# A two-layer vision-transformer tower on one core: norms and feed-forward by halves, another form of the normalising instruction, and small work moved between steps and engines

## The chip, the cores and the metric

The kernel runs on one core of a Trainium2 chip. A core has TensorE (matmuls and transposes), VectorE, ScalarE, GpSimd and SyncE, which here only issues DMAs. Each engine has its own instruction stream and runs it in order; they wait for one another on semaphores. The metric is the device time of one execution in microseconds.

## What is computed

Sixteen images of 1024 tokens, 29 features each, pass through a token embedding, a multi-head attention with a group norm in front (8 heads of 64, "layer 0"), a feed-forward with GELU, a second attention (8 heads of 16, "layer 1") and a routed feed-forward with 16 experts and a capacity of 1.2. A layer norm without weights stands before each of the four. The reference, cut to this:

```
def _layernorm(x, axis=-1, eps=1e-05):
    m = jnp.mean(x, axis=axis, keepdims=True)
    v = jnp.var(x, axis=axis, keepdims=True)
    return (x - m) / jnp.sqrt(v + eps)
...
    h = _L0_tok_ref(x, L0_tok_W)
    h = h + _L0_attn_ref(_layernorm(h, axis=-1), L0_attn_gn_w, L0_attn_gn_b, L0_attn_wq, L0_attn_bq, L0_attn_wk, L0_attn_bk, L0_attn_wv, L0_attn_bv, L0_attn_wo, L0_attn_bo)
    h = h + _L0_ffn_ref(_layernorm(h, axis=-1), L0_ffn_W1, L0_ffn_b1, L0_ffn_W2, L0_ffn_b2)
    h = h + _L1_attn_ref(_layernorm(h, axis=-1), L1_attn_Wq, L1_attn_Wk, L1_attn_Wv, L1_attn_bq, L1_attn_bk, L1_attn_bv, L1_attn_Wo, L1_attn_bo)
    h = h + _L1_ffn_ref(_layernorm(h, axis=-1), L1_ffn_switch_w, L1_ffn_switch_b, L1_ffn_expert_w, L1_ffn_expert_b)
    return h
```

## The kernel before

A batch is one image: 1024 tokens as 8 tiles of 128 tokens by 128 channels. The program is a pipeline over batches. A *segment* holds layer 0 of one batch, layer 1 of the batch before it and the routed feed-forward (`switch`) of the one before that, and near its end the embedding of the next one (`embed`). The segments are `first`, `second`, `loop` (13 executions of one hardware loop), `penult` and `final`; only `first` and `final` do one layer alone.

The clock of a segment is the *step*. A *unit* is one head and one half of the queries (512): 8 steps, one for each tile of 128 keys (`kt`). In a loop segment 32 units make 256 steps: four units of layer 0, then layer 1 and layer 0 by turns, then four of layer 1. In each step TensorE computes one tile of row maxima for a unit some 18 steps ahead (`max_tile`, L884) and one tile of scores (`scores`, L910 and L912); ScalarE takes the exponential into `pr` (L1143); VectorE reduces the tile of maxima (L1630). The maxima and the scores have two PSUM banks each. At `kt` 2, 3, 5 and 6 TensorE multiplies the exponentials of the unit before with the values. For layer 0 it does so with the high bf16 half of the exponentials (L929) and with a *low part* (L930), the difference in bf16, which `lo_parts` (L506) makes two key tiles at a time: GpSimd does it at `kt` 2, 4 and 6 and, for the last two tiles, at `kt` 0 of the next unit (`lo_done` counts them; `values0` waits for all four). GpSimd also divides the outputs by the softmax sums (`normalize`).

Everything else is *beside* work: generators (`mlp`, `embed`, `switch`, `late`, `more_heads`, `more_values`) that yield the step at which their next piece is due. Each engine runs the same generators in its own stream, so the tables `mlp_slots`, `embed_slots` and `switch_slots` set where each piece stands among the steps of every engine. The matmuls of this work share two PSUM banks (`glue`), given out by turns in the order of the tables (`glue_plan`); a piece waits until the one two before it in the plan has been read.

A norm has three pieces. VectorE takes the statistics of eight tiles (`norm_stats`: eight bn_stats, a link through a semaphore, eight bn_aggr). GpSimd makes the reciprocal root (`rstd`, L1236 and L1237: an addition and a power on 128x8). VectorE applies it (`norm_apply`, L1425: eight tensor_scalar with two scalar columns, mean and root):

```
ins = dve.tensor_scalar(dst[:, t, :], tokens[:, t, :], mv[:, s, t, 0:1], rs[:, s, t:t + 1],
                        ALU.subtract, ALU.mult)
```

Norm 0 is that of the embedding (tile `stage`, result in `on`), norms 1 and 2 those of layer 0's result and of the feed-forward's (tile `h`), norm 3 that in front of the router (tile `hm`). The result is turned on TensorE (`z_turn`, L708). In a loop segment the pieces stand at these steps: norm 3 at 24 and 27; the router's `logits` 36, `rank` 44, `place` 50 (L1593 to L1599: the weight of each token's expert, and eight instructions on `hm`); norm 0 at 184 and 187; group norm `gn` 192 to 199 (`xn`, L1475 to L1478); `copy_hm` 216; `attn0` by halves at 226 and 235 (L791; L1432 adds it to `h`); norm 1 at 236 and 238; `ffn_h` 246 and 247 (GELU, L1090); `ffn_o` 249 and 250; norm 2 at 251 and 253. `residual0` and `residual1` are additions of 128x1024 on GpSimd (L1247, L1240). L1437 makes the low part of a projection, L1449 that of a value chunk, L1620 adds an expert's result, L825 are the value matmuls of layer 1.

## Time and profile before

| | us |
|---|---|
| median of 3 runs | 6807.82 |
| lowest and highest | 6796.63, 6813.67 |
| the profiled execution, its time | 6804.59 |
| its span, first to last instruction | 6802.8 |
| mean granted TensorE clock | 0.951 of 2.4 GHz |

A window view cuts the span and gives each engine's busy time in each piece; the clock in it is the mean granted clock, where 1.00 is 2.4 GHz and 0.50 is 1.2 GHz. A wait is named as engine, tile and line that waited, then what released it. Iteration 3 is the execution of the loop segment from 1585.11 to 1994.61 us; its steps are counted by the starts of the score matmul L912, step 0 at 1585.11.

### The profile page before, as it was taken

What the parts mean: (1) busy time and instruction counts of PE and PEld (TensorE: products, weight loads), DVE (VectorE), ACT (ScalarE), POOL (GpSimd) and SP (SyncE); (2) the same over time, 40 slices, a digit from 0 to 9 for tenths busy, and PEclk for the clock granted to TensorE, in tenths of its full rate; (3) what the DMA queues carried; (4) which work ended last, traced back from release to release, by engine and by line L of the source; (5) the groups of instructions that cost most, each with busy time, mean ns of one, the idle gap of its engine ahead of it and who ended that gap; (6) DMA issues with size and microseconds to landing.
All of it is one profiled execution on the core that took longest, in us unless ns stands there. A gap on an engine that the chain in (4) does not pass through costs nothing.

```text
span 6802.8 us, 126677 instructions
## 1 busy us (share of the span) xinstructions
PE 6049.1 (89%) x40167; PEld 4017.5 (59%) x40167; DVE 4474.2 (66%) x11034; ACT 3218.6 (47%) x6321; POOL 2516.2 (37%) x2135
## 2 busy tenths in 40 slices
PE   6788898998989889898998989989898998989986
PEld 4556665665656666565665656666565665656543
DVE  4456676776757667576776767767676676767664
ACT  2345545444444444554544444454544544454531
POOL 3534433433333333333433333343333433333300
PEclk7899999999999999999999999999999999999987
DMA  2121221221122121211212222121211212222110
GB/s 59 41 67 41 58 51 29 63 51 46 46 53 49 39 52 42 59 42 38 63 42 49 49 50 49 44 50 45 59 42 38 63 34 57 49 50 44 25 30 9
DMA packets 98046, 317.01 MB, mean 47 GB/s; under 512 B 27782, under 2 KB 32854, under 8 KB 87126
## 3 DMA queue, kind: packets, MB, share of 16 engines
q1 hardware_dynamic: 97366, 308.41, 19.6%
q8 instruction: 370, 6.06, 0.4%
q14 instruction: 310, 2.54, 0.1%
HBM read 57.19 MB, written 41.94 MB: 15 GB/s over the span
## 4 chain that ended last, share of the span: by engine, by line
issue 44%; POOL 25%; PE 22%; DVE 4%; ACT 2%; DMA 2%; SPq 1%; POOLq 1%; DVEq 0%; ACTq 0%
POOL pr_lo L506 21%; PE bank L884 4%; PE bank L912 3%; PE bank L945 3%; POOL on L1265 2%; PE bank L910 2%; PE bank L870 2%; PE bank L929 2%; PE bank L930 2%; DMA stacks<-parts 1%; DVE mxh L1630 1%; PE bank L719 1%; PE bank L818 1%; PE bank L708 1%; PE bank L955 1%
## 5 line engine op out<-in xcount | busy, mean ns | idle before, releaser
L1630 DVE TENSOR_REDUCE mxh<-bank 128x1 f32<-128x512 f32 x4096 | 2789.0, 688 | 1797.3 <-PE bank L884 1779.6
L1143 ACT ACTIVATE pr<-bank 128x512 f32<-128x512 f32 x4096 | 2418.4, 598 | 2723.7 <-PE bank L912 2679.9
L884 PE MATMUL bank<-stacks 128*128 128x512 f32 x4096 | 2221.3, 543 | 348.4 <-DVE mxh L1630 233.9
L506 POOL TENSOR_TENSOR pr_lo<-pr 128x1024 bf16<-128x1024 f32 x1024 | 1944.7, 1902 | 911.4 <-ACT pr L1143 909.1
L912 PE MATMUL bank<-stacks 65*128 65x512 f32 (+1 forms) x4096 | 1673.2, 409 | 27.7 <-ACT pr L1143 27.7
L884 PEld LDWEIGHTS bank<-stacks 128*128 128x128 f32 x4096 | 799.9, 195 | 1090.2 <-DVE mxh L1630 757.7
L929 PE MATMUL bank<-v,pr 128*128 128x129 bf16 x8192 | 1063.5, 222 | 94.6 <-POOL pr_lo L506 93.3
L930 PE MATMUL bank<-v,pr_lo 128*128 128x129 bf16 x8192 | 1051.1, 220 | 0.0
L929 PEld LDWEIGHTS bank<-v,pr 128*128 128x128 bf16 x8192 | 779.5, 98 | 393.1 <-issue 346.3
L1265 POOL TENSOR_TENSOR on<-on,o_r 128x128 f32<-128x128 f32 x512 | 205.4, 401 | 2045.5 <-DVE on L1660 2045.4
L912 PEld LDWEIGHTS bank<-stacks 65*128 65x128 f32 (+1 forms) x4096 | 800.2, 195 | 261.4 <-ACT pr L1143 94.4
L910 PE MATMUL bank<-stacks 128*128 128x512 f32 x2048 | 833.3, 407 | 0.2 <-ACT pr L1143 0.2
L930 PEld LDWEIGHTS bank<-v,pr_lo 128*128 128x128 bf16 x8192 | 805.2, 98 | 0.0
L870 PE MATMUL bank<-ewT,mx 128*128 128x512 f32 x1024 | 565.2, 638 | 91.7 <-DVE hm L1620 44.8
L1620 DVE SCALAR_TENSOR_TENSOR hm<-bank,wgt,hm 128x128 f32<-128x128 f32 x2048 | 571.1, 342 | 50.7 <-PE bank L870 50.7
L945 PE MATMUL bank<-pr,v 128*32 128x512 f32 x4096 | 573.6, 636 | 0.0
L910 PEld LDWEIGHTS bank<-stacks 128*128 128x128 f32 x2048 | 401.6, 196 | 133.8 <-ACT pr L1143 90.5
L955 PEld LDWEIGHTS bank<-fold,oT 128*128 128x128 f32 x2048 | 270.6, 199 | 63.0 <-ACT oT L1160 50.5
L870 PEld LDWEIGHTS bank<-ewT,mx 128*128 128x128 f32 x1024 | 183.9, 200 | 205.6 <-DVE hm L1620 68.7
L1040 ACT ACTIVATE parts<-bank,cols 128x512 fp32r<-128x512 f32 x256 | 176.4, 689 | 224.0 <-PE bank L719 213.0
L955 PE MATMUL bank<-fold,oT 128*128 128x32 f32 x2048 | 266.3, 275 | 12.6 <-ACT oT L1160 12.6
L1273 POOL TENSOR_TENSOR on<-on,o_r 128x64 f32<-128x64 f32 x256 | 75.4, 295 | 538.1 <-DVE on L1672 538.0
(170 smaller groups left out, 4925.2 us busy)
## 6 DMA issues: line engine op xcount, KB each, us to landing
stacks<-parts SPq DMA_DIRECT2D x384, 512.0 KB, 6.5
stacks<-parts_d SPq DMA_DIRECT2D x224, 128.0 KB, 3.0
parts_d<-mx SPq DMA_DIRECT2D x16, 1024.0 KB, 4.5
stacks<-parts_d SPq DMA_DIRECT2D x224, 64.0 KB, 2.8
stage<-in_pe SPq DMA_DIRECT2D x16, 512.0 KB, 7.8
stacks<-mrow SPq DMA_DIRECT2D x512, 2.0 KB
parts_d<-on SPq DMA_DIRECT2D x16, 512.0 KB, 5.2
parts_d<-stage SPq DMA_DIRECT2D x16, 512.0 KB, 6.2
```

The costliest lines, as they stand in the source:

```text
L506: return eng.tensor_tensor(low_of(u, kt - 1).rearrange("p a b -> p (a b)"), w, hi, ALU.subtract)
L870: mm(bank[:, :], mT[:, t * P:(t + 1) * P], ewT[:, 4 * q:4 * q + 4, :].rearrange("p e f -> p (e f)"), start=True, stop=True).then_inc(fille ...
L884: mm(maxb[k % 2][:, :], qs[:, t * P:(t + 1) * P], ks[:, g * HALF:(g + 1) * HALF], start=True, stop=True).then_inc(max_filled.sem, 1)
L910: mm(bank[:, :], kA[:, head % 2, kk], qA[:, head % 2, q], start=True, stop=False)
L912: mm(bank[:, :], k_stack(layer, head)[0:last, kk], q_stack(layer, head)[0:last, q], start=(layer == 1), stop=True).then_inc(score_filled.s ...
L929: mm(dst, hi, v0[:, head // 2 % 2, kt, head % 2, 0:w], start=(kt == 0), stop=False)
L930: last = mm(dst, lo, v0[:, head // 2 % 2, kt, head % 2, 0:w], start=False, stop=(kt == T - 1))
L945: last = mm(obank[n % 2][QUAD * r:QUAD * (r + 1), :], v1[:, kt, col:col + QUAD], pr[:, at % 2, kt, :], start=(j == 0), stop=(j == 1))
L955: last = mm(obank[n % 2][:, QUAD * t:QUAD * (t + 1)], oT[:, t * P:(t + 1) * P], fold[:, :], start=True, stop=True)
L1143: act.activation(pr[:, at % 2, kt, :], score[k % 2][:, :], ACT.Exp, scale=SCALES[layer]).then_inc(exp_done.sem, 1)
L1620: ins = dve.scalar_tensor_tensor(hm[:, t, :], bank[:, e * P:(e + 1) * P], wgt[:, t, 4 * q + e:4 * q + e + 1], hm[:, t, :], ALU.mult, ALU.add)
L1630: dve.tensor_reduce(mxh[:, layer, n // 2, n % 2:n % 2 + 1], maxb[k % 2][:, :], AX_X, ALU.max)\
```

## The change

Norms and feed-forward go by halves of four tiles. `norm_stats`, `rstd` and `norm_apply` take a half `g`, and each half has its own steps. `mlp` becomes two generators, one for each half: the first half's norm 1, turn, GELU, second matmul and norm 2 stand at steps 228 to 242, the second half's at 237 to 251. Norm 0 stands at 184 and 186 (statistics, on VectorE a step later) and 188 and 190 (apply), norm 3 at 22 and 24, 26 and 28; the group norm ends at 203 instead of 199. `residual1` goes by halves as well; `copy_hm` moves from 216 to 210, `residual0` stays at 243.

The normalising instruction becomes a scalar_tensor_tensor with one scalar column (the mean); the root comes as a second tensor, one column broadcast over 128.

GpSimd's small pieces stand one or two steps later than the pieces on which they wait, and its prefix chain moves from `rank` (44) to `place` - 4 (50); `place` moves to 54. On VectorE the router's work is cut over more steps.

The last low part of each of the first four units of layer 0 in a segment (`LEADING`) moves from GpSimd to the head of the next unit's first step on VectorE, with a semaphore of its own (`lo_last`).

```diff
-    at = {"copy": -40, "oT0.3.0": -34, "attn0.0": -30, "oT0.3.1": -23, "attn0.1": -21, "ln1": -20, "z1": -18, "zT1.0": -13,
-          "zT1.1": -12, "ffn_h0": -10, "ffn_h1": -9, "ffn_o0": -7, "ffn_o1": -6, "ln2": -5, "z2": -3}
-    return {name: LAST[kind] + step for name, step in at.items()}
+    halves = ({"oT0.3": -34, "attn0": -30, "ln1": -28, "z1": -26, "zT1": -23, "ffn_h": -21, "ffn_o": -18, "ln2": -16, "z2": -14},
+              {"oT0.3": -23, "attn0": -21, "ln1": -19, "z1": -17, "zT1": -14, "ffn_h": -12, "ffn_o": -9, "ln2": -7, "z2": -5})
+    slots = {f"{name}.{g}": LAST[kind] + step for g, half in enumerate(halves) for name, step in half.items()}
+    return {"copy": LAST[kind] - 46, "res0": LAST[kind] - 13, **slots}
...
-    at = {"xT0": 179, "xT1": 180, "h0": 182, "h1": 183, "ln": 184, "z": 187, "zT0.0": 190, "zT0.1": 191, "gn": 192,
-          "gn_mean": 194, "gn_var": 197, "xn": 199, "q0.0": 204, "q0.1": 206, "k0.0": 209, "k0.1": 211, "v0c0.0": 213,
+    at = {"xT0": 179, "xT1": 180, "h0": 182, "h1": 184, "ln.0": 184, "ln.1": 186, "z.0": 188, "z.1": 190, "zT0.0": 191, "zT0.1": 193, "gn": 194,
+          "gn_mean": 196, "gn_var": 199, "xn": 203, "q0.0": 206, "q0.1": 207, "k0.0": 209, "k0.1": 211, "v0c0.0": 213,
           "v0c0.1": 215, "q1.0": 237, "q1.1": 239, "k1.0": 252, "k1.1": 254}
     return {name: LAST[kind] - 256 + step for name, step in at.items()}
...
-        at = {"oT1.0": 18, "oT1.1": 19, "attn1.0": 21, "attn1.1": 22, "ln": 24, "z": 27, "zT3.0": 31, "zT3.1": 32,
-              "logits": 36, "route": 38, "rank": 44, "place": 50, "wT0": 58, "wT1": 59, "eb0": 61, "eb1": 62}
+        at = {"oT1.0": 18, "oT1.1": 19, "attn1.0": 21, "attn1.1": 22, "ln.0": 22, "ln.1": 24, "z.0": 26, "z.1": 28, "zT3.0": 30, "zT3.1": 31,
+              "logits": 36, "route": 38, "rank": 44, "place": 54, "wT0": 59, "wT1": 60, "eb0": 62, "eb1": 63}
         first = [8 * m for m in range(8, 24)]
...
-        stats_ready = [Counts(sem(f"stats_ready{n}"), 1) for n in range(4)]
-        rstd_ready = [Counts(sem(f"rstd_ready{n}"), 1) for n in range(5)]
+        stats_ready = [Counts(sem(f"stats_ready{n}"), 2) for n in range(4)]
+        rstd_ready = [Counts(sem(f"rstd_ready{n}"), 1 if n == 4 else 2) for n in range(5)]
...
-        lo_done = Counts(sem("lo_done"), 16 * 4)
+        lo_done = Counts(sem("lo_done"), LO_DONE[-1])
+        lo_last = Counts(sem("lo_last"), LEAD)
...
-                    te.wait_ge(lo_done.sem, lo_done.at(seg.l0, 4 * (u + 1)))
+                    te.wait_ge(lo_done.sem, lo_done.at(seg.l0, LO_DONE[u + 1]))
+                    if u < LEAD:
+                        te.wait_ge(lo_last.sem, lo_last.at(seg.l0, u + 1))
...
-                    pool.wait_ge(stats_ready[n].sem, stats_ready[n].at(b, 1))
-                    s = int(n == 0)
-                    var, dst, eps, width = mv[:, s, :, 1], rs[:, s, :], pool_c[:, 1, :], T
+                    pool.wait_ge(stats_ready[n].sem, stats_ready[n].at(b, g + 1))
+                    s, ts = int(n == 0), slice(4 * g, 4 * g + 4)
+                    var, dst, eps, width = mv[:, s, ts, 1], rs[:, s, ts], pool_c[:, 1, 0:4], 4
                 link(seg, pool.tensor_tensor(dst, var, eps, ALU.add))
                 pool.tensor_tensor(dst, dst, pool_c[:, 0, 0:width], ALU.pow).then_inc(rstd_ready[n].sem, 1)
...
+            def residual1(b, g):
+                pool.wait_ge(z_ready[1].sem, z_ready[1].at(b, g + 1))
+                part = h[:, 4 * g:4 * g + 4, :]
+                biased(part, part, b2_b, 4).then_inc(res1_ready.sem, 1)
...
                 AT = switch_slots(seg.kind)
-                yield AT["ln"]
-                rstd(seg, b, 3)
-                yield AT["rank"]
+                for g in range(2):
+                    yield AT[f"ln.{g}"] + 2
+                    rstd(seg, b, 3, g=g)
+                yield AT["place"] - 4
...
+                for g in range(2):
+                    yield AT[f"ln.{g}"] + 2
+                    rstd(seg, seg.nxt, 0, g=g)
+                yield AT["gn_var"] + 2
                 rstd(seg, seg.nxt, 4)
...
+                yield AT[f"ln1.{g}"] + 1
+                rstd(seg, seg.l0, 1, g=g)
+                yield AT[f"z1.{g}"] + 1
+                residual1(seg.l0, g)
+                yield AT[f"ln2.{g}"] + 1
+                rstd(seg, seg.l0, 2, g=g)
...
+            def residuals(seg):
                 AT = mlp_slots(seg.kind)
                 yield AT["copy"]
                 if seg.l1:
                     copy_hm(seg)
-                yield AT["ln1"]
-                rstd(seg, seg.l0, 1)
-                yield AT["z1"]
-                residual1(seg.l0)
-                yield AT["zT1.0"]
+                yield AT["res0"]
                 if seg.nxt:
                     residual0(seg, seg.nxt)
...
-                    elif kt == 0 and at > 0 and units_of(seg.kind)[at - 1][0] == 0:
+                    elif kt == 0 and at > 0 and units_of(seg.kind)[at - 1][0] == 0 and units_of(seg.kind)[at - 1][1] >= LEAD:
                         lo_parts(pool, seg, at - 1, T - 1).then_inc(lo_done.sem, 1)
...
-            def norm_stats(seg, n, tokens):
+            def norm_stats(seg, n, tokens, g):
                 s = int(n == 0)
-                for t in range(T):
+                for t in range(4 * g, 4 * g + 4):
                     ins = dve.bn_stats(st[:, s, t, :], tokens[:, t, :])
                 link(seg, ins)
                 dve.memset(small[:, 7, 0:1], 0.0)
-                for t in range(T):
+                for t in range(4 * g, 4 * g + 4):
                     ins = dve.bn_aggr(mv[:, s, t, :], st[:, s, t, :])
                 ins.then_inc(stats_ready[n].sem, 1)

-            def norm_apply(b, n, tokens):
+            def norm_apply(b, n, tokens, g):
                 s, dst = int(n == 0), z0_s if n == 0 else z
-                dve.wait_ge(stats_ready[n].sem, stats_ready[n].at(b, 1))
-                dve.wait_ge(rstd_ready[n].sem, rstd_ready[n].at(b, 1))
-                for g in range(2):
-                    for j in range(4):
-                        t = 4 * g + j
-                        ins = dve.tensor_scalar(dst[:, t, :], tokens[:, t, :], mv[:, s, t, 0:1], rs[:, s, t:t + 1],
-                                                ALU.subtract, ALU.mult)
-                    ins.then_inc(z_ready[n].sem, 1)
+                dve.wait_ge(stats_ready[n].sem, stats_ready[n].at(b, g + 1))
+                dve.wait_ge(rstd_ready[n].sem, rstd_ready[n].at(b, g + 1))
+                for t in range(4 * g, 4 * g + 4):
+                    ins = dve.scalar_tensor_tensor(dst[:, t, :], tokens[:, t, :], mv[:, s, t, 0:1],
+                                                   rs[:, s, t:t + 1].broadcast_to([P, C]), ALU.subtract, ALU.mult)
+                ins.then_inc(z_ready[n].sem, 1)

...
+                yield AT[f"attn0.{g}"] + 1
+                if g == 0:
+                    dve.wait_ge(res0_ready.sem, res0_ready.at(seg.l0, 1))
+                    if seg.l1:
+                        dve.wait_ge(hm_copied.sem, hm_copied.at(seg.l1, 1))
+                add_result(seg, f"attn0.{g}", g, h, h0)
+                yield AT[f"ln1.{g}"]
+                await_drained(dve, seg, f"attn0.{g}")
+                norm_stats(seg, 1, h, g)
+                yield AT[f"z1.{g}"]
+                norm_apply(seg.l0, 1, h, g)
+                yield AT[f"ffn_o.{g}"] + 1
+                dve.wait_ge(res1_ready.sem, res1_ready.at(seg.l0, g + 1))
+                add_result(seg, f"ffn_o.{g}", g, h, h)
+                yield AT[f"ln2.{g}"]
+                await_drained(dve, seg, f"ffn_o.{g}")
+                norm_stats(seg, 2, h, g)
+                yield AT[f"z2.{g}"]
+                norm_apply(seg.l0, 2, h, g)

...
                 dve.wait_ge(prefix_ready.sem, prefix_ready.at(b, 7))
                 link(seg, dve.tensor_tensor(lg[:, :, :], oh[:, :, :], prefix[:, :, :], ALU.mult))
                 link(seg, dve.tensor_reduce(pos, lg[:, :, :], AX_X, ALU.add))
+                yield AT["place"] + 1
                 link(seg, dve.scalar_tensor_tensor(kr, pos, CAP, rp, ALU.is_lt, ALU.mult))
                 link(seg, dve.tensor_tensor(un, rp, kr, ALU.subtract))
                 dve.tensor_tensor(wgt[:, :, :], oh[:, :, :], over_e(kr), ALU.mult).then_inc(wgt_ready.sem, 1)
                 for t in range(T):
+                    if t % 4 == 0:
+                        yield AT["place"] + 2 + t // 4
                     ins = dve.scalar_tensor_tensor(hm[:, t, :], z[:, t, :], un[:, t:t + 1], hm[:, t, :], ALU.mult, ALU.add)
-                link(seg, ins)
+                    if t % 4 == 3:
+                        mark(seg, ins)
+                settle(seg)
                 for g in range(2):
                     yield AT[f"eb{g}"]
                     add_result(seg, f"{pre}eb{g}", g, hm, hm)
...
                 for step, at, layer, u, kt in steps_of(seg.kind):
+                    if kt == 0 and at > 0 and units_of(seg.kind)[at - 1] in LEADING:
+                        lo_parts(dve, seg, at - 1, T - 1).then_inc(lo_last.sem, 1)
                     tiles_due(seg, step)
...
+LEADING = [(0, u) for u in range(LEAD)]
+
+LO_DONE = [3 * min(u, LEAD) + 4 * max(u - LEAD, 0) for u in range(17)]
```

## Rows read from the trace of the kernel before

**Rows 1.** the page: busy us (share of the span) and instructions of each engine

```profile
PE 6049.1 (89%) x40167; PEld 4017.5 (59%) x40167; DVE 4474.2 (66%) x11034; ACT 3218.6 (47%) x6321; POOL 2516.2 (37%) x2135
```

**Rows 2.** windows of iteration 3: stretch, length, busy per engine, clock, DMA, GB/s

```profile
1585.11:1994.61 409.50, 371.62 (x2509) 248.30 (x2508) 279.61 (x689) 201.05 (x395) 157.34 (x133) 0.97 0.21 48
1703.02:1723.23 20.21, 20.21 (x139) 13.15 (x138) 15.84 (x41) 10.16 (x22) 8.62 (x7) 1.00 0.07 15
1624.40:1639.84 15.44, 12.26 (x109) 9.69 (x108) 14.43 (x41) 6.60 (x14) 10.06 (x8) 1.00 0.00 1
1664.02:1692.79 28.77, 25.37 (x176) 17.42 (x174) 20.22 (x43) 13.82 (x29) 10.23 (x9) 0.96 0.05 15
1860.84:1881.02 20.18, 14.66 (x62) 9.43 (x61) 15.96 (x45) 6.09 (x12) 8.37 (x8) 0.76 0.14 47
1924.99:1994.61 69.62, 55.53 (x334) 33.58 (x333) 37.20 (x110) 32.02 (x56) 14.83 (x15) 0.92 0.18 39
```

**Rows 3.** TensorE's waits in iteration 3: us in total, times, longest

```profile
PE bank L884 <- DVE mxh L1630: 14.4, 10, 5.5
...
PE bank L884 <- DMA stacks<-parts: 1.9, 1, 1.9
```

**Rows 4.** lines L1425, L1593, L1620 of the code: ns min/median/max, first and last start

```profile
L1425 DVE TENSOR_SCALAR z<-h,mv,rs x256: 337/342/348, 366.9 to 6463.0; 128x128 f32<-128x128 f32 x128
L1425 DVE TENSOR_SCALAR on<-stage,mv,rs x128: 332/336/2003, 46.5 to 5971.9; 128x128 f32<-128x128 f32 x128
...
L1593 DVE TENSOR_TENSOR lg<-oh,prefix x16: 291/1734/1744, 850.1 to 6707.5; 128x128 f32<-128x128 f32 x16
...
L1620 DVE SCALAR_TENSOR_TENSOR hm<-bank,wgt,hm x2048: 335/342/353, 880.9 to 6799.4; 128x128 f32<-128x128 f32 x187
```

**Rows 5.** groups of instructions: busy us, mean ns | idle before them

```profile
L1449 DVE TENSOR_TENSOR v<-bank,v 128x512 bf16<-128x512 f32 x128 | 87.5, 684 | 2.5 <-ACT v L1044 2.5
...
L1599 DVE SCALAR_TENSOR_TENSOR hm<-z,small,hm 128x128 f32<-128x128 f32 x128 | 35.0, 346 | 0.0
```

**Rows 6.** in order of time, steps 187 to 239: start, us, engine, line, [idle]

```profile
1866.68 6.19 DVE L1425 TENSOR_SCALAR on<-stage,mv,rs 128x128 f32<-128x128 f32 x8
...
1865.93 3.75 POOL L506 TENSOR_TENSOR pr_lo<-pr 128x1024 bf16<-128x1024 f32 x2
...
1874.56 0.79 PE L884 MATMUL bank<-stacks 128*128 128x512 f32 x1 [5.52 <-DVE mxh L1630]
...
1953.17 2.14 DVE L1425 TENSOR_SCALAR z<-h,mv,rs 128x128 f32<-128x128 f32 x8 [0.71 <-POOL rs L1237]
```

**Rows 7.** in order of time, steps 50 and 51: GpSimd, VectorE, TensorE

```profile
1665.79 1.89 POOL L506 TENSOR_TENSOR pr_lo<-pr 128x1024 bf16<-128x1024 f32 x1
...
1666.12 1.72 DVE L1593 TENSOR_TENSOR lg<-oh,prefix 128x128 f32<-128x128 f32 x1
...
1667.82 0.23 PE L929 MATMUL bank<-v,pr 128*128 128x129 bf16 x1 [2.11 <-POOL pr_lo L506]
```

**Rows 8.** in order of time, step 201: TensorE

```profile
1893.47 0.50 PE L884 MATMUL bank<-stacks 128*128 128x512 f32 x1 [1.95 <-DVE mxh L1630]
```

**Rows 9.** in order of time, step 9: TensorE

```profile
1597.99 1.16 PE L825 MATMUL bank<-wv_sb,zT 128*128 128x128 f32 x8 [0.17 <-DVE mx L1437]
```

**Rows 10.** TensorE's waits in steps 224 to 256 of iteration 3

```profile
PE bank L884 <- DVE mxh L1630: 3.0, 3, 1.5
PE bank L890 <- DVE parts L1437: 2.3, 1, 2.3
PE bank L912 <- ACT pr L1143: 1.7, 2, 1.2
PE bank L806 <- ACT mx L1090: 1.5, 1, 1.5
```

**Rows 11.** in order of time, steps 242 and 248: GpSimd, ScalarE

```profile
1957.96 2.35 POOL L1247 TENSOR_TENSOR h<-stage,on 128x1024 f32<-128x1024 f32 x1
...
1967.76 1.28 ACT L1143 ACT_TABLE_LOAD   x1
```

162 lines of the change are left out of this document (66 added, 96 removed).

## The prediction

> **What bounds the kernel now.** The page first: TensorE is busy 89% of the span, VectorE 66%, GpSimd 37% [rows 1]. That is an average over unlike stretches, so I took one execution of the main loop (iteration 3, 1585.11 to 1994.61 us, 409.5 us; 13 such executions and two cousins make most of the span), cut it at its 256 score steps and put windows over the pieces [rows 2]. In the plain steps 72 to 88 TensorE is busy 20.21 of 20.21 us at clock 1.00: nothing beside it costs anything there. The trouble is local. Steps 184 to 192, where the next batch is normalised, take 20.18 us with TensorE busy 14.66 and the clock at 0.76; steps 48 to 64 take 28.77 with 25.37 busy; steps 24 to 32 take 15.44 with VectorE busy 14.43, so there VectorE sets the pace; steps 224 to 256 take 69.62 with 55.53 busy at 0.92. TensorE's waits name the cause [rows 3]: 14.4 us for the tile maximum L1630. Tiles have two banks, so TensorE can be two tiles ahead of VectorE and no more. The bound is thus TensorE, plus each moment in which a burst on VectorE, or a late low part, outlasts that lead.
>
> **The new scalar form.** A normalising instruction on 128x128 takes 0.342 us in its median and 0.348 at most on `h`, where GpSimd is idle, but up to 2.003 on `stage` [rows 4]. Why: eight of them from 1866.68 took 6.19 us while GpSimd ran L506; eight on `h` took 2.14, so 4.05 us was standing still until L506 let go [rows 6]. The new form reads two SBUF tensors, `tokens` and the broadcast `rs`. Unhindered, its twin is L1599, a scalar_tensor_tensor from SBUF: 0.346 us [rows 5], so 0.004 x 512 = 2 us of VectorE, nothing. Does it escape the hold? Bounds: wholly (L1620, with one operand in PSUM, never over 0.353 us in 2048) or not at all (L1593, a tensor_tensor from two SBUF tensors: median 1.734, alone 0.291) [rows 4]. L1593 ended at 1667.84, 0.16 us after the L506 beside it [rows 7]. The new form has L1593's operands, so I take "not at all".
> (a) Steps 184 to 192. Of 20.18 us 5.5 are the wait for L1630 [rows 6]; clock 0.76 means 2 x 0.24 x 20.18 = 9.7 us at 1.2 GHz, worth up to 4.8 us. The halves make two bursts of four (1.05 us, 2.9 when held by one L506) with tile maxima between, which the two banks half cover. But GpSimd's order becomes low part, root, low part, root, low part, and each z half again begins when the next L506 can. Floors are VectorE's own 15.96 us with the holds kept [rows 2], 11.9 without. I take 15.7, -4.5. Bounds -1 (only the second embedding half moved) and -8.3 (20.18 to 11.9).
> (b) Steps 200 to 208. `xn` goes from step 199 to 203, where value matmuls fill TensorE while VectorE works. The wait before the tile at 1893.47 is 1.95 us [rows 8]. -1.4; bounds 0 and -1.9.
> (c) Steps 48 to 64. GpSimd stood at step 44 for the rank, so its last L506 ended at 1667.68 and TensorE waited 2.11 us for it [rows 7]. From step 50 the prefix chain has no low part behind it, as steps 48 to 55 are a layer-1 unit: -2.1 nearly sure. `place` at step 54 meets an idle GpSimd, so L1593 goes from 1.72 to 0.29 us, and its eight L1599 are split in two. Clock 0.96 over 28.77 us is 2.3 us at 1.2 GHz, worth 1.1. I take the first and the last, -3.2; bounds -2.1 and -4.6 (with L1593's 1.4).
> (d) Steps 16 to 34. Half of the `hm` statistics goes ahead to step 23, but before that TensorE waits 1.9 us for the DMA of the next stack [rows 3], issued after the maxima row of step 16, which swallows what is gained before step 21. One low part comes to VectorE at step 24, where it is nearly full [rows 2]. These cancel: 0; bounds +1.5 and -3 (VectorE rid of its holds, one and a half L506).
> (e) Last low parts of units 0 to 3 on VectorE: no row shows this there. From 0.291 us for 128 elements (L1593) and 0.684 for 512 (L1449) [rows 4, 5], 1024 make 1.21 us alone, 3.1 if held by an L506 of 1.89. It waits for the exponential of the unit's last step; queued behind it are the tile maximum and, at step 8, L1437, for which TensorE's L825 already waits 0.17 us [rows 9]. VectorE would have gone on 0.2 us earlier without it: L1437 comes 1.0 us later, +1.0. At steps 16 and 32 the low part comes about 1 us before GpSimd's and the tile maxima 1.2 us later: 0. Bounds 0 and +3.
> (f) Steps 224 to 256. Now: waits of 3.0 for tile maxima, 2.3 for L1437, 1.7 and 1.5 behind the GELU [rows 10] with a table load of 1.28 us [rows 11] before and after each half. New: the first GELU half at step 235 lies beside the attn0.1 matmuls, and w2 comes three steps after it: -1.9 of 3.2. The loads stay four. At steps 239 to 242 half bursts of both norms meet on VectorE (addition, z1.1, statistics 2.0, L1437, z2.0), so I leave the 2.3. The burst in step 254 halves and moves to 251: -0.8 and some clock, together -2.1. Against that, z2.0 is released by the same root after which GpSimd goes straight into residual0, L1247 of 2.35 us [rows 11] and an L1240 like it; with two SBUF operands z2.0 is held by the first: +2.0. copy_hm at step 210 lies in a layer-1 unit with GpSimd idle (38% busy in the loop [rows 2]), the two-instruction roots likewise: nothing. No DMA is moved. Sum -2.0; bounds +4 and -8.
> Together -4.5 - 1.4 - 3.2 + 0 + 1.0 - 2.0 = -10.1 us. 13 loops: -131. Second segment, with no switch (without c): -6.9. Penult, with no next batch (without a, b): -4.2. First and last, where a norm's chain lies open and one half can run under the other's root: -6 together, bounds 0 and -20. Total -148 from the profiled execution's 6804.59 us: 6656.5. That execution is 3.2 us under the median of 6807.82; put back, 6660.
>
> **Rivals.**
> A: the form escapes the hold, since a second operand of stride 0 may not count as a read. For it, only that L1620 is free; against, L1593. Then a is -8.3, d -2.6, f loses its +2.0: -18.5 per loop; 13 x 18.5, 21 for the two cousins and 6 are 268: 6540.
> B, no change: the holds eat the halves. a -1, b -1.4, c -2.1, e +1, f +2.7 (z2.0 held by L1247 and L1240, 4.7): -0.8 per loop: 6797.
> C, slower: the low parts stop VectorE. If each waits for an L506 (1.9) before its own 1.2, and before that for its exponential (put at 0.6), that is 3.7 us four times, 14.8 per loop against -11.1 from the other terms: +3.7, 15 times +55, with -6: 6857. It decides from 2.8 us per unit on. Against: at steps 8 and 16 GpSimd's previous L506 is over by then.
> The skill's rule on the shared interface speaks against A, as L1593 does.
>
> **Chances and range.** Forecast 0.58, A 0.20, B 0.11, C 0.11. Faster by over 0.3% (20 us, about what a measurement of this kernel can tell from no change): the forecast, A and a third of B, 0.82; within 0.3% 0.06; slower C and a little of B, 0.12. The forecast's own bounds, with terms missing in different directions, give about 6570 to 6750; the range 6540 to 6790 reaches A's time and most of the way to B, and leaves out C.
>
> **What would show it.** The normalising line's maximum on `stage`: near 1.9 us (held) or under 0.4 (A). Steps 184 to 192 near 16 us with the clock over 0.9. No L929 wait near 2 us after step 50. 64 low parts on VectorE at 1.2 us; over 2 us means C. z2.0 starting beside L1247 and held. If steps 224 to 256 still take 69 us, f was wrong; if steps 8 to 16 take over 14, e; if the clock stays at 0.76 in steps 184 to 192 although the wait shrank, half of a.

## The result and the profile after

The changed kernel takes 6751.24 us (median of 4 runs, 6740.80 to 6756.80), the kernel before 6807.56 in the same comparison: ratio 0.9916, 95% interval 0.9904 to 0.9929. It is faster, by 56 us, and inside the range, but the forecast was 148 us: by its size the prediction was wrong. The profiled execution's span is 6748.1 us at a mean clock of 0.948 (before 0.951).

The page, busy time of each engine; then windows of iteration 3 of the loop, as in [rows 2] (whole iteration, steps 8 to 16, 24 to 32, 48 to 64, 184 to 192, 224 to 256, 240 to 248):

```profile
PE 6073.5 (90%) x40167; PEld 4046.7 (60%) x40167; DVE 4525.4 (67%) x11162; ACT 3214.0 (48%) x6321; POOL 2465.6 (37%) x2215
```

```profile
1581.22:1986.76 405.54, 372.40 (x2509) 250.40 (x2508) 282.22 (x697) 200.50 (x395) 154.15 (x138) 0.97 0.21 48
1593.11:1605.79 12.68, 11.69 (x107) 9.42 (x106) 7.26 (x13) 6.35 (x13) 6.04 (x4) 1.00 0.70 197
1623.63:1640.76 17.13, 13.89 (x114) 11.55 (x112) 13.40 (x43) 7.21 (x15) 9.19 (x9) 0.90 0.00 2
...
1664.57:1691.17 26.60, 24.54 (x175) 16.90 (x174) 19.24 (x43) 13.87 (x29) 10.98 (x16) 0.99 0.06 16
...
1858.86:1876.60 17.74, 14.39 (x65) 8.05 (x64) 12.49 (x46) 5.62 (x12) 8.53 (x8) 0.90 0.15 53
...
1922.29:1986.76 64.47, 54.35 (x334) 34.87 (x333) 40.90 (x112) 32.01 (x56) 16.21 (x20) 0.93 0.19 41
1952.82:1969.59 16.77, 13.01 (x57) 7.92 (x56) 13.39 (x30) 9.68 (x15) 7.48 (x6) 0.83 0.01 2
```

The iteration fell from 409.5 to 405.5 us where 399.4 was forecast. Steps 184 to 192 took 17.7 us (20.18 before, 15.7 forecast), steps 48 to 64 26.6 (28.77), steps 224 to 256 64.5 (69.62), but steps 24 to 32 17.1 where they had taken 15.44 [rows 2]. TensorE's waits in the iteration (us in total, times, longest), to be held against [rows 3]:

```profile
PE bank L883 <- DVE mxh L1640: 14.1, 12, 3.2
...
PE bank L869 <- DVE stage L1435: 1.7, 1, 1.7
...
PE bank L742 <- DVE stage L1435: 1.1, 1, 1.1
```

The wait for the tile maximum (now L1640) didn't shrink: 14.4 before, 14.1 after. The single wait of 5.5 us in step 189 became 0.5. In its place stand 3.24 in step 25, where it had been 0.91 (and 2.02 in step 29, now gone), and 2.94 in step 244, where there was none. Two new waits name the stage addition L1435. Cut at the score steps and averaged over eleven of the 13 loop executions (the first and the last left out), a stretch at a time (us; idle is TensorE's, low is time at 1.2 GHz):

| steps | before: length, idle, low | after: length, idle, low | change | forecast |
|---|---|---|---|---|
| 0 to 16 | 23.5, 0.2, 3.3 | 24.9, 1.0, 4.6 | +1.4 | +1.0 |
| 16 to 40 | 43.3, 7.4, 0.3 | 45.4, 7.4, 6.5 | +2.1 | 0 |
| 40 to 72 | 51.8, 3.9, 4.0 | 50.3, 2.0, 4.0 | -1.5 | -3.2 |
| 176 to 200 | 43.8, 6.4, 10.2 | 42.3, 5.7, 5.9 | -1.5 | -4.5 |
| 200 to 216 | 25.2, 2.0, 0.9 | 25.0, 2.0, 0.3 | -0.3 | -1.4 |
| 224 to 256 | 68.9, 13.6, 10.7 | 64.4, 10.1, 9.0 | -4.5 | -2.0 |
| whole loop | 409.9, 37.3, 29.5 | 405.8, 32.1, 30.3 | -4.1 | -10.1 |

TensorE's idle time fell by 5.2 us a loop and its low clock not at all: it left steps 184 to 192 and turned up in steps 16 to 32. In this mean steps 184 to 192 take 18.5 us, a little more than in iteration 3. Outside the loop the second segment fell from 376.9 to 372.4 us and the last from 313.0 to 309.4, while the first (from its first score on) rose from 306.5 to 312.3 and `penult` from 399.4 to 401.0.

Then the normalising line itself (ns, minimum, median, maximum), against L1425 in [rows 4]:

```profile
L1428 DVE SCALAR_TENSOR_TENSOR z<-h,mv,rs x256: 337/346/2502, 358.8 to 6405.3; 128x128 f32<-128x128 f32 x128
L1428 DVE SCALAR_TENSOR_TENSOR on<-stage,mv,rs x128: 319/343/1059, 43.9 to 5931.6; 128x128 f32<-128x128 f32 x128
```

The maximum on `stage` is 1.06 us, neither the "near 1.9" nor the "under 0.4" of the prediction's signs, and on `h` an instruction that had never been held now stands for 2.5 us.

### The profile page after: what moved, and what is told of

It reads as the page before. It is cut to its first block, busy times and chain, and to the rows that moved or that the text cites. A ratio compares the mean times of both kernels' runs of the same rounds, so it can differ in the third digit from the quotient of the medians.

```text
span 6748.1 us, 127182 instructions
## 1 busy us (share of the span) xinstructions
PE 6073.5 (90%) x40167; PEld 4046.7 (60%) x40167; DVE 4525.4 (67%) x11162; ACT 3214.0 (48%) x6321; POOL 2465.6 (37%) x2215
## 4 chain that ended last, share of the span: by engine, by line
issue 47%; POOL 27%; PE 17%; DVE 6%; DMA 1%; POOLq 1%; ACT 1%; SPq 1%; DVEq 0%; ACTq 0%
POOL pr_lo L508 22%; PE bank L883 3%; POOL on L1264 3%; PE bank L911 2%; PE bank L869 2%; PE bank L946 2%; DVE mxh L1640 2%; PE bank L930 1%; DMA stacks<-parts 1%; PE bank L931 1%; DVE z L1428 1%; POOL rs L1235 1%; PE bank L793 1%; PE bank L909 1%; PE bank L956 1%
## 5 line engine op out<-in xcount | busy, mean ns | idle before, releaser
L1640 DVE TENSOR_REDUCE mxh<-bank 128x1 f32<-128x512 f32 x4096 | 2789.9, 687 | 1710.2 <-PE bank L883 1682.2
L508 POOL TENSOR_TENSOR pr_lo<-pr 128x1024 bf16<-128x1024 f32 x960 | 1824.3, 1901 | 1168.9 <-ACT pr L1141 1168.6
L930 PE MATMUL bank<-v,pr 128*128 128x129 bf16 x8192 | 1079.9, 224 | 54.1 <-POOL pr_lo L508 53.5
L931 PE MATMUL bank<-v,pr_lo 128*128 128x129 bf16 x8192 | 1067.7, 222 | 0.0
L1264 POOL TENSOR_TENSOR on<-on,o_r 128x128 f32<-128x128 f32 x512 | 235.3, 460 | 2015.7 <-DVE on L1670 2015.6
L869 PE MATMUL bank<-ewT,mx 128*128 128x512 f32 x1024 | 585.4, 658 | 114.1 <-DVE hm L1630 44.8
L946 PE MATMUL bank<-pr,v 128*32 128x512 f32 x4096 | 547.0, 609 | 0.0
```

The source lines that it names most:

```text
L508: return eng.tensor_tensor(low_of(u, kt - 1).rearrange("p a b -> p (a b)"), w, hi, ALU.subtract)
L869: mm(bank[:, :], mT[:, t * P:(t + 1) * P], ewT[:, 4 * q:4 * q + 4, :].rearrange("p e f -> p (e f)"), start=True, stop=True).then_inc(fille ...
L930: mm(dst, hi, v0[:, head // 2 % 2, kt, head % 2, 0:w], start=(kt == 0), stop=False)
L931: last = mm(dst, lo, v0[:, head // 2 % 2, kt, head % 2, 0:w], start=False, stop=(kt == T - 1))
L946: last = mm(obank[n % 2][QUAD * r:QUAD * (r + 1), :], v1[:, kt, col:col + QUAD], pr[:, at % 2, kt, :], start=(j == 0), stop=(j == 1))
L1640: dve.tensor_reduce(mxh[:, layer, n // 2, n % 2:n % 2 + 1], maxb[k % 2][:, :], AX_X, ALU.max)\
```

## The experiments

Times are medians of device microseconds, each with its ratio to the kernel before run beside it; a difference between two kernels is uncertain by about 15 us. The edits are to the changed kernel except in e11, e13 and e14.

### e2: the low parts back on GpSimd

```
-                    elif kt == 0 and at > 0 and ...[0] == 0 and units_of(seg.kind)[at - 1][1] >= LEAD:
+                    elif kt == 0 and at > 0 and ...[0] == 0:
...
-                    if kt == 0 and at > 0 and units_of(seg.kind)[at - 1] in LEADING:
-                        lo_parts(dve, seg, at - 1, T - 1).then_inc(lo_last.sem, 1)
```

> The changed kernel with the last low parts of units 0 to 3 back on GpSimd, all else kept. Theory (the low part on VectorE costs about what the zones 0 to 16 and 24 to 32 grew): steps 8 to 16 go from 12.7 to about 11.8 us, steps 24 to 32 from 17.3 to about 15.5 us, the wait of 3.2 us in step 25 shrinks to under 1.5, a loop loses 2.5 to 3.5 us, and the time is 6700 to 6715 us. Rival (the growth is that of the half statistics at step 23 to 25, and the low part only lies in it): steps 24 to 32 stay above 16.8 us, and the time stays at 6740 to 6755 us. A second rival, the reason for the edit: GpSimd's own low part comes later still, and the time goes up, over 6765 us.

Measured 6694.7 us, ratio 0.9828 (0.9808 to 0.9848): 57 us faster than the changed kernel. Steps 8 to 16 fell to 11.84 us, 24 to 32 to 14.53, and TensorE's low clock in steps 16 to 32 from 6.5 to 0.3 us. The theory holds, and its numbers were still too small: 6700 to 6715 us were expected. This part of the change alone costs as much as the whole change gains. Step 25 of the changed kernel, in order of time, shows how:

```profile
1624.44 0.86 DVE L1416 BATCH_NORM_STATS2 st<-hm 128x6 f32<-128x128 f32 x4
...
1625.63 0.66 DVE L1435 TENSOR_TENSOR hm<-bank,hm 128x512 f32<-128x512 f32 x1
...
1626.21 1.21 DVE L508 TENSOR_TENSOR pr_lo<-pr 128x1024 bf16<-128x1024 f32 x1
...
1627.05 2.13 POOL L508 TENSOR_TENSOR pr_lo<-pr 128x1024 bf16<-128x1024 f32 x1
...
1627.34 1.28 DVE L1640 TENSOR_REDUCE mxh<-bank 128x1 f32<-128x512 f32 x2
...
1628.08 0.50 PE L883 MATMUL bank<-stacks 128*128 128x512 f32 x1 [3.24 <-DVE mxh L1640]
```

Statistics, an addition and the low part stand one behind another on VectorE, and the tile maximum behind all three. GpSimd had stood idle for 7.5 us until 1624.60, and from there to its own low part at 1627.05 it made a division and a root, 1.6 us together. The same wait in the kernel before and in e2:

```profile
1626.53 0.50 PE L884 MATMUL bank<-stacks 128*128 128x512 f32 x1 [0.91 <-DVE mxh L1630]
```

```profile
1606.82 0.50 PE L882 MATMUL bank<-stacks 128*128 128x512 f32 x1 [2.08 <-DVE mxh L1637]
```

So the low part is worth 1.16 us of the 3.24. The 2.08 that stay, where under 1.5 were expected, lie behind half the statistics, which now come before the addition; for it the wait of 2.02 us in step 29 is gone.

### e14: the low parts on VectorE, alone, in the kernel before

```
+                    if kt == 0 and at > 0 and units_of(seg.kind)[at - 1] in LEADING:
+                        lo_parts(dve, seg, at - 1, T - 1).then_inc(lo_last.sem, 1)
```

> The kernel before with one part of the change: the last low parts of units 0 to 3 on VectorE. The prediction put it at +1.0 us a loop, all of it at step 8: 15 us, 6820 us. Theory from the undoing in the changed kernel (which gave 57 us): steps 8 to 16 +0.84, steps 24 to 32 +2 to 2.7 with a longer wait in step 24 to 26, and a low clock in steps 16 to 32 that the kernel before has not: 3 to 4 us a loop, 6850 to 6865 us. Rival (the cost in steps 24 to 32 needs the statistics by halves there): 6820 us.

Measured 6855.8 us, ratio 1.0079 (1.0066 to 1.0092): +50 us. In the mean of the loops steps 8 to 16 took 0.84 us more, 16 to 32 2.4 with 3.7 us more low clock (1.4 of it before step 24; the theory had expected 2 or more behind it), and 248 to 256 0.2. Steps 8 to 16 in the kernel before, then steps 8 to 16 and 16 to 24 in e14, and its wait in step 25:

```profile
1596.61:1608.46 11.85, 11.68 (x106) 9.41 (x105) 6.43 (x12) 6.35 (x13) 7.50 (x5) 1.00 0.71 194
```

```profile
1610.69:1623.37 12.68, 11.67 (x106) 9.41 (x105) 7.28 (x13) 6.34 (x13) 6.04 (x4) 1.00 0.70 197
1623.37:1640.98 17.61, 14.36 (x114) 11.86 (x113) 7.85 (x15) 6.34 (x14) 7.30 (x5) 0.90 0.52 114
...
1644.25 0.50 PE L885 MATMUL bank<-stacks 128*128 128x512 f32 x1 [2.06 <-DVE mxh L1633]
```

The term was mis-sized by itself and needs no half statistics to cost this much; the rival falls.

### e7: both stage additions ahead of the statistics

```
                 for g in range(2):
-                    yield AT[f"h{g}"] + 1
+                    yield AT[f"h{g}"]
                     ...
                     add_result(seg, f"{pre}h{g}", g, stage, stage)
+                for g in range(2):
                     yield AT[f"ln.{g}"] + 1
```

> The changed kernel with the two additions on stage at steps 182 and 184, both ahead of the first half's statistics (in the changed kernel the second addition stands behind them, and TensorE waits 1.12 us at step 184 and 1.70 at step 185 for the bank). Theory (these waits are an addition to the path and part of why this place gave 1.5 us a loop and not 4.5): 1.5 to 2.5 us a loop, so 6716 to 6730 us. Rival (the waits hide behind the tile maxima, which come later by as much): 6745 to 6757 us.

Measured 6692.3 us, ratio 0.9829 (0.9815 to 0.9842): 59 us faster, 4.0 us a loop, twice what was expected. The changed kernel, in order of time, steps 184 and 185; then the window of steps 184 to 192 in e7:

```profile
1859.76 0.68 DVE L1435 TENSOR_TENSOR stage<-bank,stage 128x512 f32<-128x512 f32 x1
...
1860.49 1.16 PE L742 MATMUL bank<-tokw_sb,on 29*128 29x128 f32 x8 [1.12 <-DVE stage L1435]
...
1864.73 0.86 DVE L1416 BATCH_NORM_STATS2 st<-stage 128x6 f32<-128x128 f32 x4
...
1865.92 0.66 DVE L1435 TENSOR_TENSOR stage<-bank,stage 128x512 f32<-128x512 f32 x1
...
1866.64 1.12 PE L869 MATMUL bank<-ewT,mx 128*128 128x512 f32 x2 [1.70 <-DVE stage L1435]
```

```profile
1838.12:1851.16 13.04, 12.54 (x65) 7.48 (x64) 12.01 (x45) 5.63 (x12) 8.53 (x8) 1.00 0.22 72
```

The addition empties a glue bank. The change put it a step later and, for the second half, behind the first half's statistics; the embedding matmul and an expert matmul behind it waited 2.8 us for banks, in a stretch whose clock came to 0.90. Without that the stretch takes 13.0 us at clock 1.00: less than the 15.7 of the forecast. Of the 5.4 us that this is in the mean of the loops, 2.8 are the two waits and the rest is low clock (5.9 us of it before the edit, none after). Some 1.1 us comes back as low clock in steps 200 to 208.

### e3: norm 0 and the group norm at their old steps

```
-    ... "h1": 184, "ln.0": 184, "ln.1": 186, "z.0": 188, "z.1": 190, ... "xn": 203, ...
+    ... "h1": 183, "ln.0": 184, "ln.1": 184, "z.0": 187, "z.1": 187, ... "xn": 199, ...
...
-                    yield AT[f"h{g}"] + 1
+                    yield AT[f"h{g}"]
                     ...
                     add_result(seg, f"{pre}h{g}", g, stage, stage)
-                    yield AT[f"ln.{g}"] + 1
+                for g in range(2):
+                    yield AT[f"ln.{g}"]
```

> The changed kernel with norm 0 and the group norm at their old steps (statistics at 184, both applications at 187, group norm 192 to 199), additions and roots in their old steps, low parts and the rest as changed. Theory (the zones of steps 176 to 216 give the whole worth of this part, 1.8 us a loop and not the 5.9 of the prediction): 14 times 1.8 us is 25 us, so 6776 us within 12 us, and steps 184 to 192 go back to about 20 us. Rival (the prediction's size was right and the loss came from elsewhere, the low parts or the router's steps): 14 times 5.9 is 83 us, so 6834 us. Second rival (no worth at all): 6751 us.

Measured 6771.0 us, ratio 0.9946 (0.9927 to 0.9965): the part is worth 20 us as it stands, as the theory had it. Steps 184 to 192 went back to 19.9 us. Its additions stand ahead of the statistics as well, so e7 differs from it only in the halves and the steps of this part. Between the two lie 79 us, near the forecast's 14 x 5.9 = 83 for these steps.

### e4: the feed-forward at its old steps

```
-    halves = ({... "ln1": -28, "z1": -26, "zT1": -23, "ffn_h": -21, "ffn_o": -18, "ln2": -16, "z2": -14},
+    halves = ({... "ln1": -20, "z1": -18, "zT1": -13, "ffn_h": -10, "ffn_o": -7, "ln2": -5, "z2": -3},
```

> The changed kernel with the feed-forward's pieces back at their old steps (norm 1 at 236 and 238, GELU at 246 and 247, norm 2 at 251 and 253, copy_hm at 216). Theory (steps 224 to 256 gave 4.5 us a loop in the changed kernel, most of the whole gain): 14 to 15 times 4.5 is 65 us, so 6816 us within 15 us, and steps 248 to 256 go from 17.2 to about 26 us. Rival (that zone's gain is in part the low clock's, which would come back elsewhere): under 35 us, 6775 to 6786 us.

Measured 6796.4 us, ratio 0.9979 (0.9967 to 0.9991): the part is worth 45 us, between theory and rival. Steps 248 to 256 took 26.7 us again, so the place is right. The rest of the difference to the expected 65 us lies in part in the first segment, which takes 304.4 us here and 312.3 in the changed kernel.

### e6: residual0 waits for z2.0

```
                     await_drained(pool, seg, "attn0.0", "attn0.1")
+                    pool.wait_ge(z_ready[2].sem, z_ready[2].at(seg.l0, 1))
```

> The changed kernel with residual0 on GpSimd also waiting for z2.0, the first half of norm 2. Theory (z2.0 is held by the two additions of residual0 for 3.7 us beyond its own 1.35, and TensorE waits 2.94 us in step 244 for the tile maximum behind it): L1428 z<-h takes 0.35 us each beside nothing, the wait in step 244 goes, 2 to 2.9 us a loop, 14 times, so 6710 to 6725 us. Rival (the GELU and its table load at step 244 set the pace there, so the wait changes its name): 6745 to 6755 us.

Measured 6700.6 us, ratio 0.9842 (0.9827 to 0.9856): 51 us faster, a little more than expected. The changed kernel in steps 242 to 244, then e6:

```profile
1957.15 2.38 POOL L1245 TENSOR_TENSOR h<-stage,on 128x1024 f32<-128x1024 f32 x1
...
1957.55 5.07 DVE L1428 SCALAR_TENSOR_TENSOR z<-h,mv,rs 128x128 f32<-128x128 f32 x4
...
1959.61 2.35 POOL L1238 TENSOR_TENSOR h<-h,bo_b 128x1024 f32<-128x1024 f32 x1
...
1963.28 0.50 PE L883 MATMUL bank<-stacks 128*128 128x512 f32 x1 [2.94 <-DVE mxh L1640]
```

```profile
1938.23 1.13 DVE L1429 SCALAR_TENSOR_TENSOR z<-h,mv,rs 128x128 f32<-128x128 f32 x4
...
1939.51 2.39 POOL L1246 TENSOR_TENSOR h<-stage,on 128x1024 f32<-128x1024 f32 x1 [1.65 <-DVE z L1429]
...
1945.24 0.80 PE L911 MATMUL bank<-stacks 128*128 128x512 f32 x1 [2.17 <-ACT pr L1141]
```

Two of the four normalising instructions met an addition on GpSimd, and each stood until it was over: 5.07 us instead of 1.13. With the wait added they are done first, and what limits the place next is the rival's candidate, the exponential behind a table load, 2.17 us; the 0.8 us between the two waits, the clock and the segments outside the loop make up the rest. The first segment, 306.5 us before and 312.3 in the changed kernel, takes 305.8 here. The same hold is in it (2.09 and 2.49 us for two of the four), but it accounts for part of this only: from step 120 on, where it lies, the segment takes 90.2, 94.3 and 91.2 us, and the rest is low clock in steps 0 to 96, which the edit doesn't touch.

### e8: the group norm's last instruction earlier

```
-          "gn_mean": 196, "gn_var": 199, "xn": 203, ...
+          "gn_mean": 196, "gn_var": 199, "xn": 201, ...
...
-                yield AT["gn_var"] + 2
+                yield AT["gn_var"] + 1
```

> The changed kernel with xn at step 201 and its root on GpSimd a step earlier, so that the 128x1024 instruction L1481 overlaps one low part at most. Theory (its 2.40 us instead of 0.81 hold up the tile maximum for which TensorE waits 1.20 us at step 205): the wait at 205 shrinks, 0.7 to 1.2 us a loop, 6734 to 6741 us. Rival (it is held by the low part of step 202 just as long, and VectorE now waits for the root too): 6750 to 6765 us.

Measured 6742.1 us, ratio 0.9895 (0.9880 to 0.9910), 9 us faster, in the theory's direction and smaller than can be told for certain. Steps 200 to 208 went from 12.6 to 11.9 us. In the changed kernel this line reads

```profile
L1481 DVE TENSOR_SCALAR xnT<-xnT,gsm x16: 811/2399/2409, 54.1 to 5947.3; 128x1024 f32<-128x1024 f32 x16
```

811 ns alone, 2399 in the middle: in the 14 segments where a low part runs beside it, the low part has started 0.03 to 0.05 us ahead of it; in the kernel before it started 0.2 to 0.3 us behind. In e8 it takes 811 to 815 ns in all 16.

### e5 and e13: the router's place

e5 undoes the tables in the changed kernel; e13 makes this part alone in the kernel before (its edit is shown; it also cuts VectorE's `place` over four steps).

```
-              ... "place": 50, "wT0": 58, "wT1": 59, "eb0": 61, "eb1": 62}
+              ... "place": 54, "wT0": 59, "wT1": 60, "eb0": 62, "eb1": 63}
...
-                yield AT["rank"]
+                yield AT["place"] - 4
```

> The changed kernel with the router's place at step 50, wT and eb at 58, 59, 61, 62 and GpSimd's prefix chain at step 44 again; norm 3 and all else as changed. Theory (this part is worth what steps 40 to 72 gained, 1.4 us a loop): 14 times 1.4 is 20 us, so 6771 us within 12 us; steps 48 to 56 go from 11.6 to about 13.6 us and steps 64 to 72 fall by 0.5. Rival (the prediction's 3.2 us a loop was right and another part took the rest away): 45 us, 6796 us. Second rival (nothing, since the wait only moves to step 56 and to the low clock): 6751 us.

Measured 6831.6 us, ratio 1.0032 (1.0019 to 1.0044): 80 us, more than any theory. The edit doesn't lead back to the kernel before: VectorE's half of `rank` stays a step later, so the prefix chain, again at step 44, ends later, and both low parts behind it too. In e5, steps 48 to 50:

```profile
1674.10 1.90 POOL L508 TENSOR_TENSOR pr_lo<-pr 128x1024 bf16<-128x1024 f32 x1 [0.16 <-POOL prefix L1289]
...
1676.26 1.89 POOL L508 TENSOR_TENSOR pr_lo<-pr 128x1024 bf16<-128x1024 f32 x1
...
1678.28 0.29 PE L930 MATMUL bank<-v,pr 128*128 128x129 bf16 x1 [3.05 <-POOL pr_lo L508]
```

3.05 us against 2.11 in [rows 7], and the clock fell after it: steps 48 to 56 took 16.8 us, not 13.6. So e5 doesn't size the part, and e13 was made for that.

> The kernel before with one part of the change: place at step 54, the prefix chain on GpSimd at step 50, place's pieces over four steps. The prediction put it at 3.2 us a loop: 14 times 3.2 is 45 us, 6760 us, with the low clock after it given back. Theory from the zones of the changed kernel (the wait goes, the low clock in steps 56 to 72 stays): 1.4 us a loop, 20 us, 6785 us. Steps 48 to 56 go from 13.6 to 11.6 us in both; they differ in steps 56 to 72, 25.7 us before, 24.6 by the prediction, 26.5 by the theory.

Measured 6782.0 us, ratio 0.9969 (0.9959 to 0.9980): 24 us by the medians, the theory's 20 and not the prediction's 45. Windows of steps 48 to 56 and 56 to 72, in the kernel before and in e13:

```profile
1664.02:1677.52 13.50, 11.25 (x96) 7.95 (x94) 11.47 (x26) 6.72 (x15) 4.07 (x4) 1.00 0.01 2
1677.52:1703.02 25.50, 24.34 (x167) 16.89 (x166) 16.33 (x37) 12.17 (x25) 8.68 (x7) 0.93 0.31 68
```

```profile
1660.83:1672.41 11.58, 10.96 (x95) 8.03 (x94) 7.33 (x15) 6.61 (x15) 4.04 (x10) 1.00 0.01 2
1672.41:1698.87 26.46, 25.03 (x167) 16.69 (x166) 19.72 (x48) 11.90 (x25) 8.70 (x7) 0.94 0.34 75
```

The wait goes, as forecast; the clock of the stretch behind stays low (3.7 us at 1.2 GHz in the mean of the loops before, 3.4 in e13), and that stretch grows from 25.5 to 26.5 us. VectorE has 48 instructions in it instead of 37, TensorE the same 167 matmuls; what makes it longer isn't shown.

### e1, e10, e11: the form of the normalising instruction

```
-                    ins = dve.scalar_tensor_tensor(dst[:, t, :], tokens[:, t, :], mv[:, s, t, 0:1],
-                                                   rs[:, s, t:t + 1].broadcast_to([P, C]), ALU.subtract, ALU.mult)
+                    ins = dve.tensor_scalar(dst[:, t, :], tokens[:, t, :], mv[:, s, t, 0:1], rs[:, s, t:t + 1],
+                                            ALU.subtract, ALU.mult)
```

This is e1; e10 makes the same edit to the kernel of e9, and e11 its reverse in the kernel before.

> The changed kernel with the normalising instruction in its old form, a tensor_scalar with two scalar columns. Theory (the form is neutral, both forms are held by GpSimd's additions and low parts alike): 6751 us within 12 us, and z<-h beside residual0 L1238 still takes about 2.5 us at its longest, on<-stage still has instructions of 0.35 to 2 us. Rival (the new form escapes the hold in part): the old form is held more often, over 2 us where GpSimd's L508 runs, steps 184 to 200 grow by 2 to 4 us a loop, and the time goes up by 30 to 55 us, to 6780 to 6806 us.

Measured 6776.1 us, ratio 0.9951 (0.9932 to 0.9970): 25 us slower than with the new form. Neither text had it: `z<-h` is held in both forms alike (2502 and 2503 ns at most), `z<-hm` is hardly held in either (492 ns at most in the new form, 424 in the old). The lines differ at one place. e1, then the changed kernel, in step 189:

```profile
1868.35 2.83 DVE L1428 TENSOR_SCALAR on<-stage,mv,rs 128x128 f32<-128x128 f32 x4
...
1869.20 1.89 POOL L508 TENSOR_TENSOR pr_lo<-pr 128x1024 bf16<-128x1024 f32 x1
```

```profile
1873.34 1.13 DVE L1428 SCALAR_TENSOR_TENSOR on<-stage,mv,rs 128x128 f32<-128x128 f32 x4
...
1874.20 2.03 POOL L508 TENSOR_TENSOR pr_lo<-pr 128x1024 bf16<-128x1024 f32 x1
```

GpSimd's low part starts behind the last of the four instructions, 0.06 to 0.09 us in e1 and 0.05 to 0.08 in the changed kernel. The new form keeps it off (the low part takes 2.03 us and not 1.89); the old form, although it started first, stands until the low part is over (2.83 us for four, not 1.13). It is so in 13 segments of either trace. In the mean of the loops steps 184 to 200 are 1.6 us longer in e1, and steps 200 to 208 another 1.2, with 2.5 us more low clock.

> The kernel of the four edits with the normalising instruction in its old form. Theory (the form's whole worth is one race a loop: its second instruction on stage and GpSimd's low part start within 0.1 us of each other, and the new form gets in first where the old one waits 1.7 us): 14 times 1.7 is 24 us slower than the four edits alone, if the race falls as it did; steps 188 to 192 carry all of it. Rival (the form has a general effect): z<-h and z<-hm lose too, and the difference is over 40 us. Second rival (with the additions first there is slack for it): under 8 us.

Measured 6572.6 us, ratio 0.9669, against 6569.2 for the same kernel with the new form (e9, below): 3 us. The hold is there again (steps 184 to 192 take 15.9 us instead of 13.0), but steps 192 to 200 give back 0.9, and steps 24 to 32 and 64 to 72, where the edit changes nothing, are each 0.7 us shorter, with less low clock. The second rival is nearest, though not for its reason. So the 25 us of e1 are no fixed price of the form: the same hold cost 3 here.

> The kernel before with the new form of the normalising instruction alone. Theory (a hold is not escaped by the form: in the kernel before GpSimd's low part starts 0.05 us ahead of each of these instructions, so the race is lost in either form): no change, 6808 us within 12 us, on<-stage still 1.9 to 2.0 us each. Rival (the form escapes where it can): steps 184 to 192 shrink by 2 to 4 us, 6750 to 6780 us.

Measured 6817.1 us, ratio 1.0019 (1.0011 to 1.0028): no gain, rather 0.2% slower, and why is not shown. No general escape: where the low part on GpSimd starts 0.1 us ahead, and even where it starts 0.002 to 0.010 us behind, the new form waits 2.0 us like the old.

### e12: which instructions are held

```
+            for n in range(150):
+                pool.tensor_tensor(hm[:, :, :], h[:, :, :], h[:, :, :], ALU.add).then_inc(side_pool, 1)
...
+                yield lambda: dve.tensor_scalar(dst, src, mean, root, ALU.subtract, ALU.mult)
+                yield lambda: dve.scalar_tensor_tensor(dst, src, mean, root.broadcast_to([P, C]), ALU.subtract, ALU.mult)
+                yield lambda: dve.scalar_tensor_tensor(dst, src, mean, src, ALU.subtract, ALU.mult)
+                yield lambda: dve.scalar_tensor_tensor(dst, banks[6][:, 0:P], mean, src, ALU.mult, ALU.add)
+                yield lambda: dve.tensor_copy(dst, src)
+                yield lambda: dve.bn_stats(st[:, 0, t, :], src)
```

> The changed kernel with a preamble, on tiles not yet in use: GpSimd makes 150 additions of 128x1024 one after another, and VectorE beside them 24 each of six instructions on 128x128, with 0 to 4 tiny ones between, so that they meet at all offsets: the old form, the new form, a scalar_tensor_tensor with two full SBUF operands, one with an operand in PSUM (L1630's kind), a copy, and a bn_stats. Theory (held: what reads two SBUF operands, or the old form; free: the one with PSUM, and bn_stats): the first three reach 2.4 us, the fourth and sixth stay under 0.45 us; the copy is open, 0.2 us if free. Held instructions end 0.08 us (old form) or 0.15 us (new form) after GpSimd's. Rival (stride 0 counts as no second operand): the new form reaches the fourth's time and not the third's.

In the order of that text (ns, minimum, median, maximum of 24; the preamble makes its time of 6998 us meaningless):

```profile
L1409 DVE TENSOR_SCALAR z<-h,mv,rs x24: 346/1680/1933, 33.6 to 77.6; 128x128 f32<-128x128 f32 x24
L1410 DVE SCALAR_TENSOR_TENSOR z<-h,mv,rs x24: 1432/1684/1997, 79.2 to 124.9; 128x128 f32<-128x128 f32 x24
L1411 DVE SCALAR_TENSOR_TENSOR z<-h,mv x24: 1432/1684/1934, 126.5 to 172.2; 128x128 f32<-128x128 f32 x24
L1412 DVE SCALAR_TENSOR_TENSOR z<-bank,mv,h x24: 349/351/352, 173.7 to 188.4; 128x128 f32<-128x128 f32 x24
L1413 DVE COPY z<-h x24: 617/1682/1935, 188.8 to 233.1; 128x128 f32<-128x128 f32 x24
L1414 DVE BATCH_NORM_STATS2 st<-h x24: 293/294/296, 234.7 to 248.1; 128x6 f32<-128x128 f32 x24
```

A stride of 0 changes nothing: L1410 and L1411 agree to a few nanoseconds. Held are both forms and the copy; free are the one with an operand in PSUM and the bn_stats. The maxima are 1.9 us and not the expected 2.4, as these additions take 1.89. The one instruction of 346 ns is an old form that had started 0.11 us ahead. That the form escapes is thereby excluded.

### e9: the four edits together

e2, e6, e7 and e8 in one kernel.

> The changed kernel with four edits together: last low parts of units 0 to 3 back on GpSimd, residual0 waiting for z2.0, both additions on stage ahead of the statistics, xn and its root earlier. Singly they measured about -57, -50, -59 and -9 us against the changed kernel's 6751 us. Theory (the terms lie in different stretches, so they add up): -175 us, 6576 us, and 6565 to 6600 us with what they share of the low clock. Rival (most of each gain was clock, which one edit gives back for all): over 6620 us. Steps 184 to 192 near 13.0 us, 24 to 32 near 14.5 us, 240 to 248 near 14.5 us.

Measured 6569.2 us, ratio 0.9659 (0.9647 to 0.9672): 182 us faster than the changed kernel, where the single edits add up to 176. It beats both kernels, and lies 91 us under the forecast of 6660 too, which had kept the hold on z2.0 and the low parts on VectorE. A loop takes 392.9 us with 26.5 idle and 14.0 at low clock, which had stayed near 30 in both kernels. TensorE's waits in its iteration 3:

```profile
PE bank L882 <- DVE mxh L1639: 7.9, 13, 2.1
```

## Why the prediction was wrong, point by point

The forecast gain was 148 us and the measured one 56. Two steps of it failed. Part (a) moved the norm of the embedding and put the addition that empties a glue bank at nothing: it cost 59 us (e7). Parts (d) and (e) put the low parts on VectorE at one microsecond a loop, with nothing at steps 16 and 24: they cost 3.4 us a loop, 50 to 57 us (e14, e2). Together they are about 100 us, against a miss of 92: c fell 21 us short besides, and the form and f gave 40 more than forecast. Rival B's 6797 is nearer to the measured time than the forecast's 6660.

By parts, for the whole kernel (us):

| part | forecast | measured | by |
|---|---|---|---|
| a and b, norm 0 and group norm | -83 | -20 (-79 with the additions first) | e3, e7 |
| the new form | 0 | -25 | e1 |
| c, place and prefix chain | -45 | -24 | e13 |
| d, norm 3 by halves | 0 | not taken alone | |
| e, low parts | +15 | +57 (+50 in the kernel before) | e2, e14 |
| f, feed-forward | -30 | -45 (-96 without the hold, a sum of two runs) | e4, e6 |
| first and last segment | -6 | in the others | |

The measured parts add up to -57, and the change measured -56. That they meet so closely is in part luck: each is uncertain by some 15 us, e13 was made in another kernel than the rest, and d isn't among them. By the stretches it is worth about a microsecond a loop: with the low parts back (e2) steps 16 to 32 take 30.6 us, 31.5 in the kernel before.

**What bounds the kernel.** Right as far as it goes: TensorE, plus what outlasts its lead of two tiles. The low parts (e2) and the hold on z2.0 (e6) act through that. The waits that e7 takes out are for glue banks, which the text didn't name as a bound.

**The form.** "Not at all" was right: held, by L1593's pattern, in every case in which GpSimd was first (e12). What the step left out is that a hold has two sides. It costs nothing when VectorE is first, and at one place a loop the new form was first where the old one wasn't. So the four instructions on `stage` took 1.13 and 1.35 us where the forecast had 2.9 for a held half. The Trainium skill, SBUF — State Buffer, section Who interferes with whom, says that issue order, not the kind of instruction, decides who blocks. The low part on VectorE agrees (never above 1.225 us in 64, while what GpSimd started beside it stretched, a division of 0.40 us to 1.31); step 189 of e1 doesn't: the old form started first there and lost, the new form with the same lead won. The 0.07 us estimated from the Trainium skill, VectorE: DVE Perf Modes, section Mode 2×_2P, are not seen: 0.341 us in the old form (e1) against 0.346 in the new.

**(a)** "The halves make two bursts of four ... with tile maxima between" came true: the wait of 5.5 us fell to 0.5. The step that failed is what the text left out. It moved the norm and not what stands with it in the same generator: the addition on `stage`, which empties a bank, now comes one step later for the first half and behind the statistics for the second. The tables above show `h1` moved from 183 to 184; that VectorE's part of `embed` changed too stands only in the whole kernel, and in the edit of e7, which takes it back. The wait for glue banks was in no term and in no bound. That e7 then meets the forecast for a and b is in part luck: its 13.0 us for steps 184 to 192 have hardly a hold in them, and with the hold, which the forecast kept at 15.7, they are 15.9 (e10); and against them steps 192 to 200 took 1.5 us more than before, which the forecast hadn't.

**(b)** -0.3 a loop, not -1.4: the tile wait shrank from 1.95 us (step 201) to 1.20 (step 205), and L1481, moved by four steps, fell behind a low part. e8 gives back 0.7 of it. The text sized the wait that it left and didn't ask what runs on GpSimd where it goes.

**(c)** "-2.1 nearly sure" was right, the low clock's 1.1 wasn't: e13 leaves it where it was. L1598 takes 0.28 us as said.

**(d, e)** The low part's own length was right (1.21 us, worked out from two other lines):

```profile
L508 DVE TENSOR_TENSOR pr_lo<-pr x64: 1211/1215/1225, 97.6 to 6095.9; 128x1024 bf16<-128x1024 f32 x64
```

Step 8 came out at +0.84 of the forecast 1.0, and the zero for step 32 held (steps 32 to 40 take 11.7 us before, 11.6 in e14). At step 16 the waits nearly cancelled, as the text said (0.32 and 0.84 us before, one of 1.45 in e14), but steps 16 to 24 got 3.4 us of low clock that they hadn't had. The zero for step 24 was wrong, and not for size alone: "One low part comes to VectorE at step 24, where it is nearly full", the text said, and then that it cancels. 1.2 us where VectorE already carries 14.4 of 15.4 us lands on TensorE whole: the wait in step 25 went from 0.91 to 2.06 us in e14, and from 2.08 to 3.24 between e2 and the changed kernel. e14's +3.4 a loop lies just beyond the bound of 3. It was the right row, [rows 2], and the wrong conclusion.

**(f)** -4.5 a loop by the table of stretches where -2.0 was forecast. The burst at the loop's end was worth more than 0.8: steps 248 to 256 went from 26.1 to 17.2 us. The hold on z2.0 cost more than 2.0: the forecast took residual0's first addition, the trace shows both, the second as rival B had it (4.7). Taking the hold out gave 51 us (e6), 3.0 us a loop.

**First and last.** -6 forecast. The last segment gained 3.6 us and the first lost 5.8, in part to the same hold, in part to low clock (e6).

**The rivals.** A is excluded by e12 and e11 (its sum has a slip: the two cousins give 24 us by its own terms, not 21, so 6537). C has the wrong mechanism (a low part on VectorE never waited 1.9 us) and yet the right place: of its 14.8 us a loop 3.4 were real (e14). B's reason, that holds eat the halves, was true of b and of part of f, and for c it had only the wait, -2.1, which is nearer to the 1.9 us by which e13's loops are shorter than the forecast's 3.2.

## What to carry to other kernels

When a piece moves on an engine in order, list everything in the same generator that moves with it, banks that it empties above all, and price that by who waits. Before work goes to another engine, look at the windows where that engine already fills its stretch: there the whole duration reaches the bound, and no cancelling against other terms should be booked. And don't book saved low clock wait by wait: both kernels spend some 30 us of a loop at 1.2 GHz, although the change took a wait of 5 us out; each of the large edits alone left 24 to 27, and the four together 14.0.

## What the runs showed of the hardware

- Beside GpSimd's 128x1024 additions four forms on VectorE stood until the addition ended (tensor_scalar with two columns, scalar_tensor_tensor with two SBUF operands, the same with a stride of 0, copy), and two didn't (an operand in PSUM, bn_stats; e12). VectorE's held instruction ends 0.083 us (old form, copy) or 0.147 us (new form) after GpSimd's, in each of the 96 cases of e12 but one that began ahead of it. It goes the other way too: in the changed kernel GpSimd's division of 0.40 us took 1.31 where it started 0.16 us behind VectorE's low part, and GpSimd's low part of 1.89 took 2.13 at step 25.
- A start 0.06 to 0.09 us ahead wasn't enough for the old form to be first (e1, e10); 0.10 us and more was (13 instructions on `stage` in the kernel before). For the new form 0.05 to 0.08 us was enough, and up to 0.01 us (z2.0 against L1238, and e11) wasn't. No offset between these occurred.
- 128x1024 to bf16 takes 1.21 us on VectorE and 1.89 on GpSimd.
- Low clock turned up in other stretches than the one edited: taking 5.4 us out of steps 184 to 192 (e7) brought 2.2 us of low clock to steps 200 to 208. What decides where it falls stays open.
